# Adapters that read x in a second layout, packed language data, a first FFN step per block, filler products on TensorE and some reordering in the expert stage of a two-layer adapter and mixture-of-experts kernel

## The reference, cut to what matters

```python
h = relu(x @ W1[lang] + b1[lang])                 # 256 -> 64, per block
y = x + h @ W2[lang] + b2[lang]
n = (y - mean) * rsqrt(var + 1e-5) * gamma[lang] + beta[lang]
Sm = softmax(n @ Wg.T).swapaxes(1, 2)             # 8 blocks, 8 experts, 512 tokens
G, I = top_k(Sm, 128)
out[I] += G * (gelu(n[I] @ W1e + b1e) @ W2e + b2e)
x = x + out
```

```python
h = silu(z @ w_gate[e]) * (z @ w_up[e])           # 256 -> 192
routed[token] += weight * (h @ w_down[e])         # 192 -> 256
x = x + routed + shared(z)
```

## Time and profile before

| what | value |
|---|---|
| median of three runs | 1133.94 us (1129.67 to 1136.48) |
| profiled execution, its own time | 1128.04 us |
| its span, first to last instruction | 1126.3 us |
| PE / DVE / ACT / POOL busy | 83% / 66% / 42% / 59% of the span |
| mean granted TensorE clock | 0.911 |
| HBM read / written | 115.37 MB / 43.42 MB |

### The profile page before, as it was taken

The page is one execution under the profiler, slowest core; times in us unless marked ns, Lnnn a source line. Parts: engine busy times, 40 slices in busy tenths (PEclk is TensorE's granted clock), DMA queues, the critical chain, the costliest instruction groups (busy, mean ns, idle before and its releaser), DMA issues. The chain is left out here.

```text
span 1126.3 us, 15057 instructions
## 1 busy us (share of the span) xinstructions
PE 939.8 (83%) x4616; PEld 676.5 (60%) x4616; DVE 743.0 (66%) x1523; ACT 470.3 (42%) x843; POOL 663.5 (59%) x495
## 2 busy tenths in 40 slices
PE   5981399999999999988478899998777798999960
PEld 3761289998999899973134555554454465556540
DVE  3547366766676667534578999999874786777620
ACT  2331055445544555354346665666422132233320
POOL 1113415545554555325899999999850577777870
PEclk9885599999999999998689999999876999999995
DMA  2559514444443443223212652344348599997558
GB/s 78 149 185 368 157 47 90 94 117 86 89 96 77 120 90 52 29 57 108 86 51 75 214 159 87 111 136 119 104 140 317 172 254 254 270 260 152 94 72 157
DMA packets 90455, 151.28 MB, mean 134 GB/s; under 512 B 15816, under 2 KB 72848, under 8 KB 87248
## 3 DMA queue, kind: packets, MB, share of 16 engines
q1 hardware_dynamic: 55184, 95.46, 25.9%
q0 software_dynamic: 25104, 39.86, 20.5%
q10 hardware_dynamic: 10096, 15.10, 4.1%
HBM read 115.37 MB, written 43.42 MB: 141 GB/s over the span
## 5 line engine op out<-in xcount | busy, mean ns | idle before, releaser
L628 POOL TENSOR_TENSOR wide<-wide 128x1024 f32<-128x1024 f32 x64 | 156.5, 2459 | 32.1 <-issue 32.1
L1239 DVE TENSOR_TENSOR_SCAN wide<-bank,wide 128x512 f32<-128x512 f32 x128 | 149.4, 1209 | 21.8 <-POOL wide L628 21.8
L855 ACT ACTIVATE h_raw<-bank,b 128x512 f32<-128x512 f32 x128 | 87.9, 688 | 168.3 <-PE bank L1602 165.9
L1194 DVE TENSOR_TENSOR h_lo<-h_raw,h_hi 128x512 fp32r<-128x512 f32 x128 | 87.2, 692 | 93.9 <-ACT h_hi L859 93.9
L1617 PE MATMUL bank<-w_hi,h_hi 128*128 128x256 f32 x512 | 144.3, 282 | 0.1
L1617 PE MATMUL bank<-w_lo,h_hi 128*128 128x256 f32 x512 | 142.1, 277 | 0.0
L1617 PE MATMUL bank<-w_hi,h_lo 128*128 128x256 f32 x512 | 142.0, 277 | 0.0
L602 POOL DMA_INDIRECT x_rows<-ob,put x64 | 110.9, 1733 | 27.3 <-issue 14.3
L636 POOL TENSOR_TENSOR wide<-wide 128x1024 f32<-128x1024 f32 x46 | 108.5, 2358 | 11.9 <-issue 8.2
L879 ACT ACTIVATE wide<-wide,blend 128x512 f32<-128x512 f32 x128 | 84.1, 716 | 59.9 <-POOL wide L628 56.5
L1602 PE MATMUL bank<-ex_hi,w_hi 128*128 128x512 f32 x256 | 100.3, 392 | 4.9 <-issue 4.9
(11 more groups left out here) (230 smaller groups left out, 2034.1 us busy)
## 6 DMA issues: line engine op xcount, KB each, us to landing
wide<-in_mwp SPq DMA_DIRECT2D x40, 512.0 KB, 4.4
wide<-m_rows SPq DMA_DIRECT2D x16, 1024.0 KB, 4.8
w1s<-in_fW SPq DMA_DIRECT2D x8, 1024.0 KB, 5.0
w2s<-in_fW SPq DMA_DIRECT2D x8, 1024.0 KB, 5.3
own<-in_mwp SPq DMA_DIRECT2D x15, 512.0 KB, 4.2
z_rows<-zrow SPq DMA_DIRECT2D x8, 640.0 KB, 7.1
head<-in_mwp SPq DMA_DIRECT2D x9, 512.0 KB, 4.4
xt<-in_x SPq DMA_DIRECT2D x8, 512.0 KB, 3.9
```

The costliest lines, as they stand in the source:

```text
L628: G.tensor_tensor(drive[n % DRIVES], gb[d % 2], md[d // HD][:, d % HD, :].unsqueeze(1).to_broadcast([P, CT, S]), ALU.mult).then_inc(c_u, 1)
L855: A.activation(h1_raw[f % 4][:, :], bank[:, 2 + f % 4, :], ACT.Gelu_apprx_tanh, bias=b1_0[:, bass.ds(e, 1), f]).then_inc(b_h, 1)
L1194: V.tensor_tensor(h1_lo[:, f, :], h1_raw[f % 4][:, :], h1_hi[:, f, :].bitcast(F32), ALU.subtract).then_inc(b_lo, 1)
L1239: o = V.tensor_tensor_scan(dst[:, c, :], decay[:, d:d + 1].to_broadcast([P, S]), drive[(D * b + d) % DRIVES][:, c, :], 0.0, ALU.mult, ALU.add)
```

## The change

A second input `xT` is x with tokens last, made on the host. The adapters read it straight into `xT` (two buffers), so their transposes and ScalarE's copy are gone. Both x and xT are loaded through ScalarE's queue. The language data come packed: W1 by partition in one row, W2 with b2 below it, and gamma, beta and b1 in one array `acols`; they have four buffers, and SP waits for the second product of four blocks back. ScalarE waits for the addition of block b-1 before it issues the load of x(b+1). VectorE's addition now waits for x itself.

The first step of layer 0's FFN is done block by block: POOL gathers straight by `idxT`, each block with a semaphore of its own, TensorE transposes each into a PSUM bank of its own (0, 1, 6, 7), and VectorE scales, rounds and subtracts each by itself. A helper `turn(n, count)` runs `count` products of the identity with a 512 column operand into bank n, of which nobody reads the result: 25 while VectorE makes the top-8 passes, 3 before the first block's transposes and one after each block's.

In the expert stage `ys` has six buffers instead of four, with ScalarE waiting for the scatter of six before, and rows_in(1) stands behind gate_up(0).

```diff
-        w1c = [sb(f"w1c{p}", [P, CT, AD]) for p in range(2)]
-        w2c = [sb(f"w2c{p}", [AD + 1, H]) for p in range(2)]
-        b1c = [sb(f"b1c{p}", [AD, 1]) for p in range(2)]
-        xT = sb("xT", [P, CT, S])
+        w1c = [sb(f"w1c{i}", [P, CT, AD]) for i in range(4)]
+        w2c = [sb(f"w2c{i}", [AD + 1, H]) for i in range(4)]
+        xT = [sb(f"xT{p}", [P, CT, S]) for p in range(2)]
...
-        ys = [sb(f"ys{i}", [P, H]) for i in range(4)]
+        ys = [sb(f"ys{i}", [P, H]) for i in range(6)]
...
-                h, p = divmod(b, 2)
-                sp.wait_ge(a_y, level(b - 2))
+                i = b % 4
+                sp.wait_ge(a_ad, level(b - 4))
                 lang = sp.value_load(t["ids"][0:1, b:b + 1], min_val=0, max_val=LANGS - 1)
-                sp.dma_start(xt[p][:, :, :], x_rows[b * S:(b + 1) * S, :].rearrange("(t p) c -> p t c", p=P)).then_inc(a_x[p], 16)
-                sp.dma_start(w1c[p][:, :, :], t["aW1"].rearrange("l (c p) a -> l p c a", p=P)[bass.ds(lang, 1), :, :, :].rearrange("l p c a -> (l p) c a")).then_inc(a_in[p], 16)
-                sp.dma_start(w2c[p][0:AD, :], t["aW2"][bass.ds(lang, 1), :, :].rearrange("l a c -> (l a) c")).then_inc(a_in[p], 16)
-                sp.dma_start(w2c[p][AD:AD + 1, :], t["ab2"][bass.ds(lang, 1), :]).then_inc(a_in[p], 16)
-                sp.dma_start(b1c[p][:, :], t["ab1"][bass.ds(lang, 1), :].rearrange("l a -> a l")).then_inc(a_in[p], 16)
-                sp.dma_start(gam0[:, b, :], t["agam"][bass.ds(lang, 1), :, :].rearrange("l p c -> (l p) c")).then_inc(a_in[p], 16)
-                sp.dma_start(bet0[:, b, :], t["abet"][bass.ds(lang, 1), :, :].rearrange("l p c -> (l p) c")).then_inc(a_in[p], 16)
+                sp.dma_start(w1c[i][:, :, :].rearrange("p c a -> p (c a)"), t["aW1"][bass.ds(lang, 1), :, :].rearrange("l p a -> (l p) a")).then_inc(a_in[i], 16)
+                sp.dma_start(lang_cols[:, b, :], t["acols"][bass.ds(lang, 1), :, :].rearrange("l p c -> (l p) c")).then_inc(a_in[i], 16)
+                sp.dma_start(w2c[i][:, :], t["aW2"][bass.ds(lang, 1), :, :].rearrange("l a c -> (l a) c")).then_inc(a_in[i], 16)
...
+            def b_gather_first():
+                for j in range(4):
+                    G.indirect_dma_start(xg0[0][:, j, :], None, n0_rows[:, :],
+                                         bass.IndirectOffsetOnAxis(ap=idxT[:, j, 0:1], axis=0)).then_inc(b_first[j], 16)
...
-            b_gather(0, 0)
+            b_gather_first()
+            pool.sem_inc(b_take, 1)
             b_gather(0, 1)
...
-                                     ys[e % 4][:, :], None, compute_op=ALU.add).then_inc(e_put[e % 2], 16)
+                                     ys[e % 6][:, :], None, compute_op=ALU.add).then_inc(e_put[e % 2], 16)
...
-            def a_xT_out(b):
-                act.wait_ge(a_xTm, level(b))
-                act.wait_ge(a_hm, level(b - 1))
-                A.activation(xT[:, :, :], two(0), ACT.Copy).then_inc(a_xT, 1)
+            def load_xT(b):
+                act.dma_start(xT[b % 2][:, :, :], t["xT"][b, :, :].rearrange("(c p) s -> p c s", p=P)).then_inc(a_xin[b % 2], 16)
+            def load_x(b):
+                act.dma_start(xt[b % 2][:, :, :], x_rows[b * S:(b + 1) * S, :].rearrange("(t p) c -> p t c", p=P)).then_inc(a_x[b % 2], 16)
+            load_xT(0)
+            load_x(0)
+            load_xT(1)
+            load_x(1)
...
-                A.activation(hT[0:AD, :], bank[0:AD, 2, :], ACT.Relu, bias=b1c[b % 2][:, :]).then_inc(a_h, 1)
+                A.activation(hT[0:AD, :], bank[0:AD, 2, :], ACT.Relu, bias=lang_cols[0:AD, b, 2 * CT:2 * CT + 1]).then_inc(a_h, 1)
...
-            a_xT_out(0)
             for b in range(B):
                 a_front(b)
-                if b + 1 < B:
-                    a_xT_out(b + 1)
+                if b + 2 < B:
+                    load_xT(b + 2)
+                if 0 < b < B - 1:
+                    act.wait_ge(a_y, level(b - 1))
+                    load_x(b + 1)
...
-                wait_moved(act, e_put[e % 2], e // 2 - 2, 16)
-                A.activation(ys[e % 4][:, :], bank[:, 6 + e % 2, H:2 * H], ACT.Copy).then_inc(e_ys, 1)
+                wait_moved(act, e_put[e % 2], e // 2 - 3, 16)
+                A.activation(ys[e % 6][:, :], bank[:, 6 + e % 2, H:2 * H], ACT.Copy).then_inc(e_ys, 1)
...
+                dve.wait_ge(a_x[p], level(b // 2, 16))
...
+            def b_exT_first():
+                for j in range(4):
+                    at = slice(j * P, (j + 1) * P)
+                    if j < 3:
+                        dve.wait_ge(b_T0, j + 1)
+                    else:
+                        dve.wait_ge(b_T, level(0))
+                    for c in range(CT):
+                        o = V.tensor_scalar(ex_raw[:, c, at], bank[:, (0, 1, 6, 7)[j], c * P:(c + 1) * P], gam0[:, j, c:c + 1], bet0[:, j, c:c + 1],
+                                            ALU.mult, ALU.add)
+                    if j == 3:
+                        o.then_inc(b_xraw, 1)
+                    dve.drain()
+                    V.tensor_copy(ex_hi[0][:, :, at], ex_raw[:, :, at])
+                    dve.drain()
+                    o = V.tensor_tensor(ex_lo[0][:, :, at], ex_raw[:, :, at], ex_hi[0][:, :, at].bitcast(F32), ALU.subtract)
+                o.then_inc(b_exT, 1)
+            b_exT_first()
...
-            def a_xT_in(b):
-                p = b % 2
-                pe.wait_ge(a_x[p], level(b // 2, 16))
-                pe.wait_ge(a_xT, level(b - 1))
-                for c in range(CT):
-                    for j in range(TT):
-                        o = T.transpose(bank[:, c, j * P:(j + 1) * P], xt[p][:, j, c * P:(c + 1) * P], ident[:, :])
-                o.then_inc(a_xTm, 1)
             def a_hidden(b):
                 p = b % 2
-                pe.wait_ge(a_in[p], level(b // 2, 16 * 6))
-                pe.wait_ge(a_xT, level(b))
+                pe.wait_ge(a_in[b % 4], level(b // 4, 16 * 3))
+                pe.wait_ge(a_xin[p], level(b // 2, 16))
                 pe.wait_ge(a_h, level(b - 1))
                 for c in range(CT):
-                    o = T.matmul(bank[0:AD, 2, :], w1c[p][:, c, :], xT[:, c, :], start=(c == 0), stop=(c == CT - 1))
+                    o = T.matmul(bank[0:AD, 2, :], w1c[b % 4][:, c, :], xT[p][:, c, :], start=(c == 0), stop=(c == CT - 1))
                 o.then_inc(a_hm, 1)
...
-                    a_xT_in(b + 1)
...
+            def turn(n, count):
+                for _ in range(count):
+                    T.matmul(bank[:, n, :], ident[:, :], flip[:, :].unsqueeze(1).to_broadcast([P, 4, P]), start=True, stop=True)
+            turn(5, 25)
...
-                        b_T_in(s + 1, 1 - p, 2 * g + (r + 1) // 2)
+                        b_T_in(s + 1, 1 - p, 2 * g + (r + 1) // 2 - p)
...
-            b_T_in(0, 0, 0)
+            def b_T_first():
+                turn(5, 3)
+                for j in range(4):
+                    pe.wait_ge(b_first[j], 16)
+                    for c in range(CT):
+                        o = T.transpose(bank[:, (0, 1, 6, 7)[j], c * P:(c + 1) * P], xg0[0][:, j, c * P:(c + 1) * P], ident[:, :])
+                    o.then_inc(b_T0 if j < 3 else b_T, 1)
+                    turn(5, 1)
+            b_T_first()
...
-            rows_in(1)
             for e in range(E1 + 2):
                 if e < E1:
                     gate_up(e)
+                if e == 0:
+                    rows_in(1)
```

28 lines of the change are left out of this document (18 added, 10 removed), and 5 rows, old and new, of the table LAYOUT.

## The result

The changed kernel takes 1124.99 us (median of 20 runs, 1121.38 to 1132.11); the kernel before, in 20 runs beside it, 1133.70 us (1125.73 to 1139.78). The ratio is 0.9928, with a 95% interval of 0.9911 to 0.9946: 8.2 us less, between 6.1 and 10.1, where the forecast said 18.1. The direction was right and the range held the time, but half of the gain is missing. In all ratios and medians here, executions more than 1.5% above the fastest of their kernel are left out (two of e16's six, one of e17's six and one of e18's twelve). The profiled execution took 1121.38 us with a span of 1119.6 us, against 1128.04 and 1126.3 before.

The account below looks back on a forecast made before the run. TensorE was taken to pace the adapters, a serial chain to follow, POOL to bound the last stage. Terms -12.5 - 0.8 - 5.0 - 1.7 + 1.9 = -18.1 us gave 1116 us against the median, range 1105 to 1127.

Parts of the forecast that it names:

- Start: Adapters' first hidden product: starts near 8.0 us instead of 11.41, gain 3.4 us, bounds 2.4 to 4.2.
- A round: Adapter rounds: without x transposes and copy wait, 6.5 us instead of 8.03, seven rounds gain 10.7 us.
- Bytes: Adapter DMA: 15.8 MB of transfers nearly fill the stage, costing 1.6 us of the gain, within 0 and 6.
- rival A: Adapters: transfers set the pace, eighth addition stays at 74 us, median 1128; chance 0.15 shared with another rival.
- The adapters in sum: Adapter stage: start and round gains less the transfer cost, 3.4 + 10.7 - 1.6 = 12.5 us gained.
- Routing tail: After the top-8 passes: fillers keep full clock, small transposes and flips halve; gain 0.8 us, bounds -1 to 1.
- first step per block: Table of indices to first FFN product: dropped list copy and blockwise work gain 5.0 us, bounds 1.7 and 6.
- clock: First FFN, 135 to 140 us: fillers between blocks remove half-clock loss; gain 1.7 us, bounds 0 and 1.7.
- Rival B: Top-8 stretch: TensorE never leaves half clock, fillers make lists 19.5 us late, median 1141; chance 0.05.
- Second row behind the gate product: Expert stage: row 1 transposed later delays POOL's gather, loss 1.9 us, bounds 0 and 2.5.
- Six ys buffers: Expert stage: extra buffers leave the scatter chain as long, 0 us, bounds -3 and +1.

Follow-up runs that it names:

- e16: Changed kernel with row 1 transposed ahead of the first gate product and four ys buffers instead of six; median 1119.38 us, ratio 0.9871 to the kernel before.
- e17: Changed kernel with second block's loads held, row 1 ahead of the gate product, two fillers per adapter round and four ys buffers; ratio 0.9829 to the kernel before.
- e18: Changed kernel with row 1 transposed ahead of the first gate product, six ys buffers kept; median 1121.03 us, ratio 0.9899 to the kernel before.
- e1: Changed kernel with ScalarE requesting the second block only after the first block's language data landed; one run, first hidden product at 9.41 us, time not compared.
- e6: Changed kernel with SP requesting the first FFN weights only after the eighth block's second product; one run, eighth addition at 74.39 us, time not compared.
- e13: Kernel before with the adapter part of the change alone; median 1124.66 us, ratio 0.9941 to the kernel before.
- e9: Kernel before with the blockwise first FFN step and its fillers alone; median 1122.61 us, ratio 0.9922 to the kernel before.
- e4: Changed kernel with row 1's transposes put back ahead of the first gate product; one run, fifth gather 11.95 us after the first, time not compared.
- e7: Changed kernel with all `turn` filler calls taken out; one run, seven adapter rounds in 46.8 us, time not compared.
- e15: Changed kernel with second block's loads held, row 1 first, two fillers per adapter round and more in early TensorE waits; median 1116.18 us, ratio 0.9860 to before.
- e11: Changed kernel with second block's loads held, row 1 ahead of the gate product and no adapter fillers; median 1118.89 us, ratio 0.9909 to the kernel before.
- e3: Changed kernel with eight dummy identity transposes per adapter round in place of those removed; one run, eighth addition at 68.48 us, time not compared.

## Why the prediction was half right

- *Start, -3.4 us.* Wrong: -0.25. The step names the three language loads but prices only the landing of one x load; the product waits for the last of the three, and that lands behind the second block's 1 MB. e1 shows 1.75 us of it; the other 1.4 are not settled.
- *A round, 7 x 1.53 = -10.7 us.* This is the step that failed, in its size. Its full-clock arithmetic was right (6.44 us against 6.5). But 8.03 us, from which it subtracted, held slow rounds, and the 6.5 assumed that none would be left; the working says itself that the difference of 7.7 to 8.03 "lies in rounds at half clock" and then lets it vanish. At full clock the gain is 7.65 - 6.44 = 1.21 a round, 8.5 us. In nine traces whose adapters have the changed code and no filler (without e6) the seven rounds come to 46.8 to 54.4 us, 51.6 on average (52.1 with e6), and in the two with the code of before to 56.2 and 58.2: the gain is 5.5 us, an estimate, with only two traces on one side of it. The rest went to half clock: what the seven rounds take above full clock grew from 57.2 (the mean of the two) - 7 x 7.65 = 3.6 us to 51.6 - 7 x 6.44 = 6.5.
- *Bytes, +1.6 us, and rival A.* Not there. Rounds of 6.80 us beside a full DMA share, and no gain from taking the weights away (e6), exclude them there. Where transfers did cost time is the start. (The issue time of 0.39 us that the working takes from the earlier trace rows stands there as 0.45; nothing hangs on it.)
- *The adapters in sum, -12.5 us.* By the eighth addition -2.0 in the changed kernel's own trace, by the averages above 0.25 + 5.5 = 5.8, in e13 by the ratio -6.7 (3.5 to 9.7). The profiled execution of the changed kernel met a bad one of the patterns (rounds of 9.30 and 9.23 us).
- *Routing tail -0.8, first step per block -5.0, clock -1.7: -7.5 us.* Right by the ratio: e9 gives -8.8 (5.6 to 12.1) for the three. The changed kernel's marks give 5.9, e9's own 3.5. Of the 5.9 the index transposes gave 0.3 instead of 0.8, the clock 1.6 instead of 1.7, and the first step 4.0 instead of 5.0, since VectorE needs 1.6 us a block and not 1.45 and is the bound from the first block on. Rival B falls: 25 fillers took 23.48 us in a gap that had been 24.54.
- *Second row behind the gate product, +1.9 us.* Right: the fifth gather came 1.99 us later, and e4 takes it back.
- *Six ys buffers, 0 us.* Right that they give nothing, for the reason named: POOL's wait went from ys to the landing. The bound of +1 on the other side may be too small.

The parts measured, -6.7 - 8.8 + 2, give -13.5 us, the whole -8.2 (6.1 to 10.1). With 2 us for the buffers it is -11.5, and the rest lies within the intervals of the parts, 3 us each; it is not settled beyond that. By marks of the traces in place of ratios, and the averages for the rounds, the sum is -0.25 - 5.5 - 5.9 + 1.9 = -9.7 us, and -7.7 with the buffers' 2; the -8.2 lies between. Of the 9.9 us that the forecast had too much, the rounds are then 5.2 and the start 3.2. The range held the time because it reached far enough toward a smaller gain, not because the sum was right.

What stays open is why the clock falls when it does, and so why the changed adapters lose more to it than those of before. Shown is that the slow rounds are rounds at a lower clock, that transfers do not make them, and that the same code gives between 0.78 (e6) and 0.90 (e7, corrected) from 18 to 64 us. In five of six kernels with two fillers a round the last three rounds or more are all 6.80 us; e15 is the sixth, with two.

## What to carry to other kernels

When a change takes work off the engine that sets the pace, and that engine runs at half clock part of the time, cost the rounds at both levels and count how often each occurs, before and after; a mean that holds slow rounds is no base from which to subtract full-clock arithmetic. Order the first loads by who waits for them, across all queues: a small load behind megabytes that nobody needs yet sets the start. A wait's name in the profile is not its cause: ask what else ends at that moment, before adding buffers against it. And a single trace can be off in a stage by as much as the change is worth there (here 46.8 to 54.4 us for the same seven rounds), so compare stages over several.

## What the runs showed of the hardware

- TensorE's granted clock can fall without a gap in its work: in e15 its rows show no gap over 0.33 us from 18.99 us on, and the clock is 1.00 from 20 to 25 us and 0.50 from 30 to 35. The Trainium skill ("TensorE: Matmul & The Clock Gate", HAM oscillation — how this bites in real kernels) ties such falls to idle gaps of the engine; this trace does not agree.
- Which rounds are slow comes in patterns: e11's rounds (6.07, 6.85, 7.44, 9.31, 7.54, 6.44, 7.47 us) are those of e4 (6.07, 6.84, 7.42, 9.31, 7.57, 6.44, 7.44), and others differ by up to 7.6 us in the sum with the same code (46.8 in e7, 54.4 in the changed kernel).
- Eight transposes more in each round did not lower the clock in the one trace of them (0.96 in e3); all rounds but the first two and one of 8.94 us took 7.32 us.
